# Loading, turning and folding the slice weights during the edge stage instead of among the last MLP layers

## What is computed

```python
aggr = segment_sum(edge_attr_256, dst, N)                  # edges sorted by dst
h = relu(concat([layernorm(x), aggr]) @ W1 + b1)
h = relu(h @ W2 + b2)
x = x + h @ W3 + b3
xn = layernorm(x)
x_mid = (xn @ W_x + b_x).reshape(N, H, D)
temp = clip(temperature, 0.1, 5.0)
slice_weights = softmax((x_mid @ W_slice + b_slice) / temp)  # N x H x G
token = (xn @ W_fx + b_fx) summed with slice_weights over the nodes, divided by their sum
out_slice = attention among the 64 tokens of each head (W_q, W_k, W_v)
x = x + (slice_weights @ out_slice) @ W_out + b_out
```

## Time and profile before

| | us |
|---|---|
| median of 3 runs | 639.31 (638.81 to 640.17) |
| the profiled execution, its own time | 640.71 |
| its span, first to last instruction | 638.9 |
| TensorE busy | 596.8 (93%) |
| VectorE busy | 374.5 (59%) |
| ScalarE busy | 304.6 (48%) |
| POOL busy | 229.7 (36%) |
| mean granted TensorE clock | 0.986 of full speed |

### The profile page before, as it was taken

How to read it: one execution, slowest core, us unless ns; L and a number is a source line. 1 busy time by engine, 2 the same in 40 slices (tenths; PEclk the granted TensorE clock), 3 DMA queues, 4 the chain that set the end, 5 groups by cost and what they waited for, 6 DMA issues and landing times.

```text
span 638.9 us, 11434 instructions
## 1 busy us (share of the span) xinstructions
PE 596.8 (93%) x3433; PEld 357.9 (56%) x3433; DVE 374.5 (59%) x1040; ACT 304.6 (48%) x449; POOL 229.7 (36%) x303
## 2 busy tenths in 40 slices
PE   5679999969998999999899899999999998999997
PEld 2345555634555555554469544444444444888885
DVE  6745445333475656656357888788888887322221
ACT  5145656522212222232122366666766656777772
POOL 4345565600000000000042666666666664595000
PEclk9799999988999999999999999999999999999999
DMA  8999999999999999999110035334334343011112
GB/s 302 375 400 395 403 403 408 388 346 341 353 372 359 384 381 363 380 365 339 41 48 33 18 66 75 74 66 81 67 67 81 66 76 72 26 74 74 74 74 81
DMA packets 104842, 134.02 MB, mean 210 GB/s; under 512 B 57339, under 2 KB 59345, under 8 KB 104805
## 3 DMA queue, kind: packets, MB, share of 16 engines
q1 hardware_dynamic: 103989, 133.29, 61.8%
q10 hardware_dynamic: 816, 0.26, 0.2%
HBM read 114.29 MB, written 6.40 MB: 189 GB/s over the span
## 4 chain that ended last, share of the span: by engine, by line
PE 75%; DMA 19%; DVE 2%; issue 1%; SPq 1%; POOL 0%; ACT 0%; DVEq 0%
DMA ring_mem<-edge_attr_in 19%; PE ps L1602 13%; PE ps L1510 13%; PE ps L1534 12%; PE ps L1253 12%; PE ps L1289 7%; PE ps L1374 7%; PE ps L1295 6%; PE ps L1284 2%; PE ps L1494 2%; SPq L414 1%; PE ps L1366 0%; DVE ring_mem L1128 0%; DVE ring_mem L1126 0%; PE ps L1589 0%
## 5 line engine op out<-in xcount | busy, mean ns | idle before, releaser
L999 DVE TENSOR_TENSOR big<-big,ps 128x64 f32 x319 | 70.8, 222 | 102.1 <-PE ps L1284 58.6
L1253 PE MATMUL ps<-ring_mem,side 128*32 128x256 f32 (+1 forms) x1596 | 103.6, 396 | 25.9 <-DMA ring_mem<-edge_attr_in 25.8
L1534 PE MATMUL ps<-side,ring_mem 128*128 128x512 f32 x196 | 92.4, 593 | 1.8 <-ACT ring_mem L763 1.8
L1253 PEld LDWEIGHTS ps<-ring_mem,side 128*32 128x32 f32 (+1 forms) x1596 | 51.5, 113 | 62.9 <-issue 36.4
L1602 PE MATMUL ps<-side,ring_mem 128*128 128x256 f32 x360 | 77.9, 379 | 0.0
L1602 PEld LDWEIGHTS ps<-side,ring_mem 128*128 128x128 f32 x360 | 68.4, 190 | 9.3
L653 POOL TENSOR_TENSOR ring_mem<-ring_mem 128x512 f32<-128x512 f32 x48 | 61.3, 1277 | 30.1 <-DVE ring_mem L1140 30.1
L839 ACT ACTIVATE ring_mem<-big 128x1024 uint16 (+1 forms) x45 | 60.6, 1357 | 15.6 <-PE ps L1602 15.6
L716 ACT ACTIVATE side<-ps 128x512 f32<-128x512 f32 (+1 forms) x50 | 25.6, 512 | 85.0 <-PE ps L1253 84.9
L613 POOL MEMSET ring_mem<- 128x128 f32 x1 | 0.2, 204 | 181.3 <-PE ps L1253 181.3
L1534 PEld LDWEIGHTS ps<-side,ring_mem 128*128 128x128 f32 x196 | 37.0, 190 | 47.9 <-issue 43.8
(11 more groups left out here) (143 smaller groups left out, 825.0 us busy)
## 6 DMA issues: line engine op xcount, KB each, us to landing
ring_mem<-edge_attr_in SPq DMA_DIRECT2D x84, 1024.0 KB, 8.5
ring_mem<-edge_attr_in SPq DMA_DIRECT2D x62, 256.0 KB, 4.9
x_sb<-x_in SPq DMA_DIRECT2D x16, 384.0 KB, 5.9
result<-x_sb SPq DMA_DIRECT2D x16, 384.0 KB
big<-side SPq DMA_TRANSPOSE x49, 3.1
side<-L_gnn_W_in SPq DMA_DIRECT2D x2, 256.0 KB, 6.4
ring_mem<-L_ffn_W_x_in SPq DMA_DIRECT2D x2, 256.0 KB, 3.1
ring_mem<-L_ffn_W_out_in SPq DMA_DIRECT2D x1, 512.0 KB, 3.8
```

Of the source, the lines that this page charges most:

```text
L999: dve.tensor_tensor(win, win, found[:, :, q * WINDOW:(q + 1) * WINDOW], ALU.add).then_inc(groups_added, 1)
L1253: return mm(ps[q * WINDOW:(q + 1) * WINDOW, SUM_BANKS[h], col:col + F], lhsT=hot[0:parts, h * 2 + j, t, :], rhs=ring8[0:parts, h * 2 + j, ...
L1534: last = mm(ps[:, s % 2, :], lhsT=xn_t[:, s % 2, k, :], rhs=wc[:, k, :], start=(k == 0), stop=(k == KF - 1))
```

## The change

The loads of the fold go from behind the last chunk to batch 21 of SP's program, right behind the load of W3. POOL's clearing goes along, waiting for `h1x_psum` instead of the last chunk. TensorE turns W_x in batch 25, behind that batch's layer 3 and ahead of its `turn`; ScalarE copies the result in batch 25; TensorE waits for that copy in batch 26, behind its sums and ahead of its layer 1. VectorE makes the inverse temperature and the repeated b_x in batch 26. TensorE makes the products in batch 29, and VectorE scales them there. `fold_biases` stays among the last layers. The late weights no longer wait for the transposes. W_x, its turned form and `wc` now lie in `xn`, the small fold tiles in `ln_t`, and the first four normalised tiles of the softmax stage in `side` instead of `xn`.

```diff
+TURN_WX_AT, FOLD_WX_AT = 25, 29
...
+        wx = [xn_mem[:, k * 512:(k + 1) * 512] for k in range(KF)]
+        wx_t = xn_mem.rearrange("p (k j n) -> p k j n", k=KF, j=PAIRS)
+        wc = xn_mem.rearrange("p (k n) -> p k n", k=KF)
+        soft_xn = side[:, 0:1024].rearrange("p (b f) -> p b f", b=UNROLL)
...
                 if isinstance(b, int) and b == 2 * X_TRIPS + 1:
                     sp.wait_ge(h1x_psum, TRIPLES + 1)
                     sp.dma_start(w3_sb[:, :, :], w3.rearrange("(k p) n -> p k n", p=P)).then_inc(w3_in, 16)
+                    for k in range(KF):
+                        sp.dma_start(wx[k], w_x[k * P:(k + 1) * P, :]).then_inc(wx_in, 16)
+                    sp.dma_start(bx_col, b_x.rearrange("(j p) -> p j", p=P), allow_slow_non_contiguous=True).then_inc(fold_in, 16)
+                    sp.dma_start(bsl_bc, b_slice.rearrange("(a g) -> a g", a=1).broadcast_to([P, G])).then_inc(fold_in, 16)
+                    sp.dma_start(temp_bc, temperature.rearrange("a h b c -> a (h b c)").broadcast_to([P, H])
+                                 ).then_inc(fold_in, 16)
+                    sp.wait_ge(blk_clear, 1)
+                    for hh in range(2):
+                        sp.dma_start(blk_s[hh * D:(hh + 1) * D, hh * G:(hh + 1) * G], w_slice).then_inc(fold_in, 16)
...
             sp.wait_ge(win_psum, CHUNKS)
-            for k in range(KF):
-                sp.dma_start(wx[k], w_x[k * P:(k + 1) * P, :]).then_inc(wx_in, 16)
...
-            sp.wait_ge(fold_t, 1)
             sp.dma_start(wout_sb, w_out.rearrange("(j p) n -> p j n", p=P)).then_inc(late_in, 16)
...
-            pool.wait_ge(win_psum, CHUNKS)
+            pool.wait_ge(h1x_psum, TRIPLES + 1)
             pool.memset(blk_s, 0.0).then_inc(blk_clear, 1)
...
+                if isinstance(b, int) and b == TURN_WX_AT:
+                    act.wait_ge(fold_t, 1)
+                    for k in range(KF):
+                        act.activation(wx_t[:, k].rearrange("p j n -> p (j n)"), ps[:, bank_of(b + 1) + k, :], ACT.Copy
+                                       ).then_inc(wx_ready, 1)
...
+                if isinstance(b, int) and b == FOLD_WX_AT:
+                    dve.wait_ge(fold_t, 2)
+                    for k in range(KF):
+                        fold_step(dve.tensor_tensor(heads(wc[:, k, :]), heads(ps[:, bank_of(b) + k, :]), inv_all, ALU.mult))
...
+                if isinstance(b, int) and b == TURN_WX_AT + 1:
+                    dve.wait_ge(fold_in, 16 * 5)
+                    dve.wait_ge(fold_v, fold_step(dve.tensor_scalar(inv_temp, temp_bc, 0.1, 5.0, ALU.max, ALU.min)))
+                    fold_step(dve.reciprocal(inv_temp, inv_temp))
+                    fold_step(dve.tensor_copy(bx_rep, bx_col.unsqueeze(2).broadcast_to([P, PAIRS, P])))
...
+                if isinstance(b, int) and b == TURN_WX_AT + 1:
+                    pe.wait_ge(wx_ready, KF)
...
+                if isinstance(b, int) and b == TURN_WX_AT:
+
+                    banks_free(b + 1)
+                    turn_wx(bank_of(b + 1))
+                if isinstance(b, int) and b == FOLD_WX_AT:
+                    banks_free(b)
+                    fold_wx(bank_of(b))
                 turn(b, h, groups)
...
             full_layer3(i + 1, 4)
-            fold_transposes()
             pe.wait_ge(h1e_added, 2 * MLP_CHUNKS + 1)
...
             full_layer3(i + 3, 4)
-            fold_weights()
```

More of the change, by code:

```diff
@@ L199, in build @@
         k_t = part(1792, 256)
-        more_xn = part(0, 1024).rearrange("p (b f) -> p b f", b=UNROLL)
-        def normed(s):
-            return xn[:, s, :] if s < UNROLL else more_xn[:, s - UNROLL, :]
         ones = part(7936, P // 2)
@@ L220, in build @@
         win_sb = side[:, 2048:3072].rearrange("p (b n) -> p b n", b=2)
-        wc = side[:, 0:1024].rearrange("p (k n) -> p k n", k=KF)
         w2_sb = side[:, 1024:1536].rearrange("p (k n) -> p k n", k=KF)
@@ L231, in build @@
         vw = xn[:, :, :]
+        xn_mem = xn[:, :, :].rearrange("p b f -> p (b f)")
+        wx = [xn_mem[:, k * 512:(k + 1) * 512] for k in range(KF)]
+        wx_t = xn_mem.rearrange("p (k j n) -> p k j n", k=KF, j=PAIRS)
+        wc = xn_mem.rearrange("p (k n) -> p k n", k=KF)
+        soft_xn = side[:, 0:1024].rearrange("p (b f) -> p b f", b=UNROLL)
         ln_t = sb("ln_t", [P, KF, X_NODES])
@@ L235, in build, with normed @@
         w3_sb = w1a_sb
[L237 to L240, removed]
+        more_xn = part(0, 1024).rearrange("p (b f) -> p b f", b=UNROLL)
+        def normed(s):
+            return soft_xn[:, s, :] if s < UNROLL else more_xn[:, s - UNROLL, :]
+        ln_mem = ln_t[:, :, :].rearrange("p k n -> p (k n)")
+        bx_rep = ln_mem[:, 256:768].rearrange("p (j n) -> p j n", j=PAIRS)
+        fold_mem = ln_mem[:, 0:256]
         blk_s = fold_mem[:, 0:128]
@@ L629, in _ @@
             rstd(0, 0, FIRST, FIRST)
-            pool.wait_ge(fold_t, 1)
+            pool.wait_ge(l3_psum, L3_TRIPLES + 1)
             pool.memset(wqkv, 0.0).then_inc(late_clear, 1)
@@ L747, in _ @@
             relu_one(MLP_CHUNKS, P)
-            act.wait_ge(fold_t, 1)
-            for k in range(KF):
-                act.activation(wx_t[:, k].rearrange("p j n -> p (j n)"), ps[:, 2 + k, :], ACT.Copy).then_inc(wx_ready, 1)
             relu_two(MLP_CHUNKS - 1, 4 * P, [ps[:, m, :] for m in range(KF)])
@@ L970, in residual_stats, with heads, fold_step @@
                 stats(i, n, bn2_done, seen, mv2_ready)
+            def heads(v):
+                return v.rearrange("p (h g) -> p h g", h=H)
+            folded = [0]
+            def fold_step(ins):
+                ins.then_inc(fold_v, 1)
+                folded[0] += 1
+                return folded[0]
+            inv_all = inv_temp.unsqueeze(2).broadcast_to([P, H, G])
             def batch(b, h, i, groups, parts, what):
@@ L1083, in full_residual @@
                 residual_stats(i, i, X_TILES, i * X_TILES + X_TILES)
[L1085 to L1093, removed]
             full_residual(L3_TRIPLES, 4)
@@ L1098, in _ @@
             full_residual(L3_TRIPLES + 1, 4)
[L1099 to L1103, removed]
             full_residual(L3_TRIPLES + 2, 6)
             full_residual(L3_TRIPLES + 3, 4)
-            dve.wait_ge(fold_t, 2)
-            for k in range(KF):
-                fold_step(dve.tensor_tensor(heads(wc[:, k, :]), heads(ps[:, 2 + k, :]), inv_all, ALU.mult))
             full_residual(L3_TRIPLES + 4, 6)
@@ L1308, in banks_free, with turn_wx, fold_wx @@
                     pe.wait_ge(x2_ready, L3_AT[b - 2] + 1)
+                elif b - 2 == FOLD_WX_AT:
+                    pe.wait_ge(fold_v, 5)
+            def turn_wx(bank):
+                pe.wait_ge(wx_in, 16 * KF)
+                for k in range(KF):
+                    for j in range(PAIRS):
+                        last = tr(ps[:, bank + k, j * P:(j + 1) * P], wx[k][:, j * P:(j + 1) * P], ident[:, :])
+                last.then_inc(fold_t, 1)
+            def fold_wx(bank):
+                pe.wait_ge(wx_ready, KF)
+                pe.wait_ge(fold_in, 16 * 5)
+                for j in range(PAIRS):
+                    for k in range(KF):
+                        last = mm(ps[:, bank + k, j * P:(j + 1) * P], lhsT=wx_t[:, k, j, :], rhs=blk_s, start=True, stop=True)
+                last.then_inc(fold_t, 1)
             def hidden_ready(i):
@@ L1431, in full_layer3 @@
                 third_layer(i, X_TILES, bank).then_inc(l3_psum, 1)
[L1433 to L1447, removed]
             def fold_biases():
```

## The result

The changed kernel takes 635.91 us (median of 14 runs, 634.78 to 638.4) against 639.33 us (14 runs, 636.27 to 643.9). The ratio is 0.9949 with a 95% interval of 0.9933 to 0.9965: faster by 2.2 to 4.3 us. Measured again beside other kernels, twice, the ratio was 0.9966 (0.9946 to 0.9985) and 0.9962 (0.9945 to 0.998). The mean of the three ratios is 0.9959, a gain of 2.6 us. The forecast was 2.0; the 637.3 us named lies above the first median by 1.4 us, and its range began at 636.5, so the result lies 0.6 us outside it. The two later ratios, put on the 639.31 us that the forecast started from, would give 637.1 and 636.9, inside the range: the miss is small, and part of it may be the spread of the measurements.

A forecast was written before the change was run, and what follows sets the result against it. TensorE bounds the kernel (75% of the chain, DMA 19%), with full DMA queues in the edge stage. -2.65 + 0.65 = -2.0 us, from 639.31 to 637.3 us; range 636.5 to 639.1.

The forecast's parts named there:

- the shift of the edge stage: Edge stage: TensorE's added work and the DMA queue act in parallel, the larger counts; about 0.65 us later, bounds 0.55 and 1.28.
- Term 1: Last MLP layers: transposes (0.87 us) and products (1.78) leave TensorE's chain and count in full, -2.65 us.
- Term 2: TensorE in batches 25 to 30: 2.65 us of moved work less about 1.9 of waiting filled, shift about 0.6 us.
- lower bound of 0.55: Edge stage: smallest shift allowed, the 2.65 us of moved work less all TensorE waiting there.
- Term 3: DMA queue, seven loads ahead of chunk 44: 2.1 us of DMA time, less a 1.44 us pause, leaves 0.66.
- the middle that I took: DMA queue: 2.1 us for the seven loads, between bounds of 1.43 and 2.72.
- the upper end: DMA queue: the seven loads cost at most 2.72 us, all DMA time between 309 and 317 us.
- The pause: DMA engines' last pause, 153 to 156 us: 1.44 us idle, expected to absorb that much of the loads' time.
- Of the rivals the first: DMA queue costs its upper end or more: shift 1.28 us, chunk 45 0.2 late, 637.9 us or above; chance 0.20.
- the layers kept pace on VectorE: Rival, last layers: VectorE falls behind, gain 0.87 instead of 2.65 us, time 639.1; chance 0.08.
- SP was not stuck: Rival, between W3 and chunk 44: small loads hold SP, TensorE 5.5 us late, 642.8 up to 644.5 us; chance 0.03.
- the small loads did not stop the queue one by one: Last rival, DMA queue: about 2 us for each of five small loads, 10 us lost, slower by several us; chance 0.01.

The follow-up runs named there:

- e5: Kernel before, with only the seven fold loads moved on SP, to behind the first layer 3 after batch 49; 637.76 us against 639.0, ratio 0.9977.
- e6: Changed kernel with the seven loads issued a second time in the old place, into a part of the ring nothing reads; 638.07 us, ratio 0.998 to before.
- e8: Changed kernel with only the two loads of W_x issued a second time with the last chunk; no time given, the whole gap is back.
- e9: Changed kernel with only the five small loads issued a second time with the last chunk; no time given, gap 0.73 us.
- e1: Kernel before with the seven loads early, behind W3, and the fold's transposes, copies, products and scaling left among the last layers; ratio 1.0009 to before.
- e7: Changed kernel with the seven early loads issued behind chunks 46 and 47 (batch 23) instead of behind W3; 636.11 us, ratio 0.9949 to before.
- e4: Changed kernel run again unchanged for a second profile; ratio 0.9966 to before.

## Why the prediction was wrong in its size

Its mechanism stands: work taken off TensorE among the last layers, filled into its waits in the edge stage, at a price in the DMA queue. The step that failed is a term that the sum left at nothing without a reason: what it saves to take the seven loads away from behind the last chunk. It was 1.27 us by the gaps. The second error went the other way, the shift of the edge stage, forecast 0.65 and in fact 1.2 to 1.45.

**Term 1, -2.65 us.** Right. From the first layer 3 behind batch 49 to the logits of tile 1 it took 314.99 to 358.04 = 43.05 us before, and 313.80 to 354.07 = 40.27 in the third profile of the changed kernel: 2.78 less.

**The missing term, about -1.3 us.** The prediction prices the seven loads where they arrive and not where they leave; no engine waits for them there. They stood in the way of TensorE's code. The gaps of the changed kernel are 0.0, 0.51 and 0.64 (mean 0.38) against 1.65 and 1.66, so 1.27 us; moving the loads alone gave 1.5 in time (0.3 to 2.6). The sign was in the trace: the chain has 1.65 us of "issue" at 313.33, in the same stretch in which the loads ran. The range did hold 0.8 us for the spread and "for a saving that I missed"; this one was larger.

**Term 2, TensorE in the edge stage, forecast 0.55 to 0.65.** The two additions (+0.87, +1.05) and the filled wait of batch 29 are right. Wrong is that all waiting would be used up. (The lower bound of 0.55 does not follow from the rows either: 2.65 less the 1.90 and 0.14 us of idle time in the earlier trace rows is 0.61.) Idle time of TensorE from 150 us to the last turning, as its timelines mark it: 1.90, 2.44 and 1.51 us in three profiles with the fold late (before twice, e5), mean 1.95; and 1.24, 0.55, 0.88, 1.06, 0.0 and 0.83 in six with all of it early (the changed kernel three times, e6, e8, e9), mean 0.76. So 1.2 us are filled, not 1.9 to 2.0, and the shift is 2.65 - 1.2 = 1.45 us; against the two profiles of the kernel before alone (mean 2.17) it is 1.2. Measured directly, from the start of batch 22 to the end of the last turning, it takes 161.0, 161.4 and 160.2 us in the three and 163.0, 162.0, 162.3, 163.0, 161.8 and 163.0 in the six, a difference of 1.65 on the means, or 1.3 against the kernel before alone.

**Term 3, the queue, 2.1 us of DMA time of which 0.66 was to be left.** Chunk 45 landed 6.17, 6.13 and 6.13 us behind chunk 43 with the loads late, and 9.05, 8.10, 8.49, 8.66, 8.62 and 8.63 in those six profiles: 2.4 us later, halfway between the middle that I took and the upper end. Chunk 45 was to come 0.4 us in time; it was late by 1.24 and 0.55 us in two of the three profiles of the changed kernel, and in the third batch 30 waited 0.88 for its chunk. Chunk 61, the second of batch 30, landed 53.07 and 52.63 us behind chunk 43 in the two profiles of the kernel before, 51.74 in e5, and on the mean of the six 53.97. So 1.1 us are left against the kernel before, and 1.5 if e5 is counted in, instead of 0.66. The pause thus swallowed about 1.3 us where there was one, near the 1.44 counted; in e5 there was hardly any (DMA share 0.99 in 153 to 156 us, against 0.52 and 0.74 in the two of the kernel before), so what it swallows is not the same in every execution. The loads alone do not contradict this: e1 against e5, which differ in the place of the loads and neither of which has them at the branch, is 0.0032 in the ratio or 2.0 us, but the two were measured on different chips, and their intervals allow about 0.4 to 3.6.

**The sum with these sizes.** -2.78 - 1.27 + 1.45 = -2.6 us (-2.8 with the shift of 1.2), and the mean of the three measured ratios is 2.6. So the forecast of 2.0 came as near as it did by luck: a saving of 1.3 us that was missed, and a price put 0.6 to 0.8 us too low, partly cancelled. Of the rivals the first was right in its place (batch 22) and near in its size (a shift of 1.28), though the time did not show it. The others fell: the layers kept pace on VectorE, SP was not stuck, and the small loads did not stop the queue one by one, so the trace does not agree with the 2 us for each that the prediction estimated from the Trainium skill. Taking them out of the place ahead of chunk 45 was worth 8.6 - 7.5 = 1.1 us of the queue, though, for some 70 KB, where W_x with its 0.5 MB has the other 1.4. That is far more than their share of the bytes. To that degree the rule of the Trainium skill, page "DMA: Bandwidth & Descriptors", section "Rules for kernel authors", that transfers under 64 KB are mostly overhead, is borne out.

What stays open: the first comparison (3.3 us by the ratio) lies above the sum of the sizes by 0.7, within its interval. TensorE's clock does not explain it: in 140 to 150 us, where it had waited for edges before, it was granted 0.50, 0.66 and 0.83 in the three profiles with the loads late, and 0.71 and five times 0.66 in the six, so a spell at 1.2 GHz there is longer or shorter from one execution to the next, and on the means (0.66 and 0.67) the change does not shorten it.

## What to carry to other kernels

A stretch of "issue" in the chain behind a branch is not a constant of the program. If a large transfer is under way just before it, the code may come late, and holding that transfer back for a few us can be worth as much as moving the work: here the gap gave 1.27 us, and the work moved 2.78 less a shift of 1.2 to 1.45. Loads that are put into a nearly full queue are not free because of one pause: of 2.4 us 1.1 to 1.5 were left here, and a later place (e7) only moved the wait. Take along only what is needed there, and give small pieces that are needed late a place of their own. And before a sum is made, every idle stretch of the bounding engine near a removed instruction deserves a line, even if nothing seems to wait for what is removed.

## What the runs showed of the hardware

Two loads of 256 KB, which no engine was waiting for, delayed the code behind a branch: TensorE stood still for 1.65 to 1.75 us with them in four profiles (before twice, e6, and e8 with W_x alone), and in the ten profiles without them there, e9 with the small loads among them, for 0.0 to 0.74. A load of 512 KB whose packets began behind the fetch did not do it (e4: 310.61 against 311.34, gap 0.51). The time from the start of the fetch (16 KB) to the first matmul behind it was 2.5 to 3.0 us in 13 of the 14 profiles. And SP, with many small loads behind large ones and edges under way, needed up to 2.28 us for the issue of a single load (b_slice), where the same load took 0.51 in the old place, behind W_x but without edges.
